# Moving the transposes of q and k behind the output product, with their PSUM banks and waits, in a one-core attention and feed-forward kernel

## What is computed

```python
def _L0_attn_ref(hidden_states, w_qkv, q_ln_w, q_ln_b, k_ln_w, k_ln_b, w_out):   # 128 batches of 32 positions
    qkv = jnp.clip(jnp.einsum('bsd,ed->bse', hidden_states, w_qkv), -8.0, 8.0)
    q, k, v = jnp.split(qkv, 3, axis=-1)
    q, k = _layer_norm(q, q_ln_w, q_ln_b), _layer_norm(k, k_ln_w, k_ln_b)
    ...                                              # 32 heads of 16
    scores = jnp.einsum('bqhd,bkhd->bhqk', q, k) * scale
    probs = jax.nn.softmax(jnp.where(causal, scores + alibi_bias, -inf), axis=-1)
    attn = jnp.einsum('bhqk,bkhd->bqhd', probs, v).reshape(B, S, D)
    return jnp.einsum('bsd,ed->bse', attn, w_out)

x = x + attention(einsum('bct,bcd->bdt', x, style_weights[style_ids]))   # per batch 32x32 mixing first
x = x + ffn(einsum('bsi,boi->bso', x, adapter_weights[adapter_ids]))     # one 512x512 adapter per batch
# ffn: relu(x up)^2 down, plus (sum of the best two gate logits) * x route, then a layer norm
```

## Time and profile before

| | us |
|---|---|
| median of 3 runs | 1124.7 |
| lowest and highest run | 1123.63, 1128.38 |
| the profiled execution, device time | 1129.65 |
| its span (first to last instruction) | 1127.9 |
| TensorE matmuls busy | 1083.4 (96%) |
| weight loads, DVE, ACT, POOL busy | 876.0, 676.3, 600.6, 713.8 |
| mean granted TensorE clock | 0.990 |

### The profile page before, as it was taken

One profiled execution on the slowest core, in us unless ns is written; L12 is line 12 of the kernel. 1 busy time (PEld: TensorE's weight loads), 2 busy tenths in 40 slices (PEclk: granted clock), 3 DMA queues, 4 the chain that ended last, 5 costly groups with the idle time before them and its releaser, 6 DMA issues.

```text
span 1127.9 us, 28302 instructions
## 1 busy us (share of the span) xinstructions
PE 1083.4 (96%) x11396; PEld 876.0 (78%) x11396; DVE 676.3 (60%) x1040; ACT 600.6 (53%) x985; POOL 713.8 (63%) x612
## 2 busy tenths in 40 slices
PE   5999999999999999999989999999999999999994
PEld 3877778788887888788767778787878888787883
DVE  5567667676666667666667245565556565554432
ACT  4466767676766777777767424435261624333220
POOL 4566878788888787878666463556455464433342
PEclk9999999999999999999999999999999999999997
DMA  7125555556554556565567953232414224030101
GB/s 276 41 78 182 183 187 180 169 168 220 173 195 158 198 171 229 170 214 170 175 215 233 350 184 105 84 94 92 126 49 125 67 86 102 28 85 28 47 28 38
DMA packets 95296, 160.84 MB, mean 143 GB/s; under 512 B 46400, under 2 KB 47168, under 8 KB 89792
## 3 DMA queue, kind: packets, MB, share of 16 engines
q1 hardware_dynamic: 79456, 118.16, 32.5%
q0 software_dynamic: 12224, 34.10, 9.5%
q10 hardware_dynamic: 3488, 6.78, 1.7%
HBM read 93.97 MB, written 42.47 MB: 121 GB/s over the span
## 4 chain that ended last, share of the span: by engine, by line
PE 93%; issue 2%; DMA 1%; POOL 1%; DVE 1%; ACT 0%; SPq 0%; POOLq 0%; DVEq 0%; ACTq 0%
PE banks L675 16%; PE banks L860 16%; PE pair L884 15%; PE bank L724 8%; PE bank L675 7%; PE bank L790 7%; PE banks L877 4%; PE bank L877 4%; PE banks L790 3%; PE bank L665 3%; PE pair L692 3%; PE pair L752 2%; PE banks L830 1%; PE banks L735 1%; PE banks L771 1%
## 5 line engine op out<-in xcount | busy, mean ns | idle before, releaser
L1752 POOL TENSOR_TENSOR w_lo<-w2t,w_hi 128x2048 fp32r<-128x2048 f32 x38 | 174.8, 4600 | 39.4 <-ACT w_hi L1053 39.3
L1822 POOL TENSOR_TENSOR u_lo<-act,u_hi 128x512 fp32r<-128x512 f32 x64 | 82.7, 1293 | 102.4 <-ACT u_hi L1253 102.2
L675 PE MATMUL banks<-wqkv_hi,h_hi 128*128 128x512 f32 x256 | 104.7, 409 | 0.2
L860 PE MATMUL banks<-yT_hi,up_hi 128*128 128x512 f32 x256 | 100.8, 394 | 0.0
L675 PE MATMUL banks<-wqkv_hi,h_lo 128*128 128x512 f32 x256 | 100.7, 393 | 0.0
L675 PE MATMUL banks<-wqkv_lo,h_hi 128*128 128x512 f32 x256 | 100.6, 393 | 0.0
L860 PE MATMUL banks<-yT_hi,up_lo 128*128 128x512 f32 x256 | 99.8, 390 | 0.0
L860 PE MATMUL banks<-yT_lo,up_hi 128*128 128x512 f32 x256 | 99.7, 389 | 0.0
L884 PE MATMUL pair<-down_lo,u_hi 128*128 128x512 f32 x256 | 99.6, 389 | 0.0
L884 PE MATMUL pair<-down_hi,u_hi 128*128 128x512 f32 x256 | 99.6, 389 | 0.0
L884 PE MATMUL pair<-down_hi,u_lo 128*128 128x512 f32 x256 | 99.6, 389 | 0.0
(11 more groups left out here) (217 smaller groups left out, 3048.1 us busy)
## 6 DMA issues: line engine op xcount, KB each, us to landing
w2t<-in_w SPq DMA_DIRECT2D x38, 1024.0 KB
vx<-v_hl SPq DMA_DIRECT2D x128, 68.0 KB
x1g<-x_rows SPq DMA_DIRECT2D x32, 256.0 KB, 2.9
kx<-k_hl SPq DMA_DIRECT2D x124, 64.0 KB
x_rows<-x1t SPq DMA_DIRECT2D x31, 256.0 KB, 3.5
ffn_high<-w_high SPq DMA_DIRECT2D x20, 256.0 KB, 3.3
ffn_low<-w_low SPq DMA_DIRECT2D x20, 256.0 KB, 3.4
stage<-in_wqkv SPq DMA_DIRECT2D x3, 1024.0 KB, 8.2
```

The costliest lines, as they stand in the source:

```text
L675: m = e.matmul(into, a[:, c, :], b[:, n, c, :], start=(c == 0 and k == 0), stop=(c == KC - 1 and k == 2))
L860: i = e.matmul((B2, B3)[n % 2], a[:, w, cols], b[m % 2][:, c, :], start=(c == 0 and k == 0), stop=(c == KC - 1 and k == 2))
L1752: e.tensor_tensor(w2_lo[:, :, :], w2t[:, :, :], w2_hi[:, :, :].bitcast(F32), ALU.subtract).then_inc(d_wlo, 1)
L1822: e.tensor_tensor(u_lo[n % FC][:, :], act[n % 2][:, :], u_hi[n % FC][:, :].bitcast(F32), ALU.subtract) \
```

## The change

For the tiles in halves (5 to 29):

- TensorE turns q and k of tile i - 1 behind `out_project(i - 4)` and ahead of `values(i - 3)`.
- The homes in PSUM are exchanged: q and k go to banks47, the slot and the attention's output to banks23. The chunk's detour goes from B4 to B6.
- ACT normalizes q and k later (behind `high_h`), and scales and splits them at the pass's end, k first, with the rounding of the next slot's adapter behind them.
- DVE takes the low parts one pass later, behind the first statistics and ahead of `take_k`; SP spreads k one pass later, behind the spread of v and the store of x1. `low_planes`, `join_planes` and `high_planes` go later in the pass, and SP's stores and loads of planes go behind the load of the adapter.
- `project_q`, `project_k`, `project_v` no longer wait for low parts of q and k in halves; `turn_slot` waits for `ck` (k of tile i is taken out of its bank), `style` waits for the chunk's low part.

TensorE, pass 9, before: steps behind the projections (`xg` is the slot, `on` the attention's output, `w2` the adapter, `wo` the output weights).

```diff
-    turned_values = banks47[:, :, KC * HALF:2 * KC * HALF]
+    turned_slot = half(banks23, 0)
+    turned_values = banks23[:, :, KC * HALF:2 * KC * HALF]
     def q_at(t):
-        return half(banks23, 0) if in_halves(t) else whole(B7 if t == T - 1 else B3)
+        return half(banks47, 0) if in_halves(t) else whole(B7 if t == T - 1 else B3)
...
 SP loop
+                if in_halves(i - 2):
+                    spread_k(i - 2)
                 if 0 <= i - 5 < CHUNKS:
                     keep_chunk(i - 5)
+                if 0 <= i - 4 < CHUNKS:
+                    load_chunk(i - 4)
+                if i >= 5:
+                    load_w2(i - 5)
                 if i >= T - 8:
                     keep_planes(i - T + 8)
...
-                if i >= 1:
+                if i >= 1 and not in_halves(i - 1):
                     spread_k(i - 1)
...
 TensorE
             def project_q(i):
                 upto(e, "cq", i - 1)
-                if in_halves(i - 2):
-                    upto(e, "qlo", i - 2)
-                    upto(e, "klo", i - 2)
+                if i > LAG:
+                    e.wait_ge(d_tl, i - LAG)
+                    upto(e, "olo", i - 5)
...
                 if i >= LAG:
-                    turn_slot(i - LAG, banks47)
+                    turn_slot(i - LAG, banks23)
                 if i >= 4:
                     turn_values(i - 4)
-                if i >= 1:
+                if i >= 1 and not in_halves(i - 1):
                     turn_q(i - 1)
                     turn_k(i - 1)
...
                 if i >= 4:
                     out_project(i - 4)
+                if in_halves(i - 1):
+                    turn_q(i - 1)
+                    turn_k(i - 1)
                 if i >= 3:
                     values(i - 3)
...
 ACT loop
-                if i >= 1:
+                if i >= 1 and not in_halves(i - 1):
                     normalize(i - 1)
...
                 if i >= SHORT:
                     high_h(i + 1)
+                if i >= T - 8:
+                    join_planes(i - T + 8)
+                    high_planes(i - T + 8)
+                if in_halves(i - 1):
+                    normalize(i - 1)
...
                 if i >= 2:
                     soft_exp(i - 2)
+                if in_halves(i - 1):
+                    scale_k(i - 1)
+                    scale_q(i - 1)
+                    high_k(i - 1, k_hl)
+                    high_q(i - 1)
+                    high_w2(i + 1 - LAG)
...
 DVE loop
                 stats_of(i, 0, qn, "cq")
-                if 0 <= i - 5 < CHUNKS:
-                    low_chunk(i - 5)
-                if i >= T - 8:
-                    low_planes(i - T + 8)
+                if in_halves(i - 2):
+                    low_k(i - 2, k_hl)
+                    low_q(i - 2)
                 take_k(i)
                 stats_of(i, 1, kn, "ck")
                 aggregate(i)
+                if 0 <= i - 5 < CHUNKS:
+                    low_chunk(i - 5)
```

More of the change, by code:

```diff
@@ L763, in turn_slot @@
                     e.wait_ge(d_tl, s)
[L764 removed]
+                if slot_halved(s):
+                    upto(e, "ck", s + LAG)
                     upto(e, "olo", s + LAG - 5)
[L766 removed]
+                elif s == LAST:
+                    upto(e, "qlo", T - 3)
+                    upto(e, "klo", T - 3)
                 for c in range(KC):
@@ L770, in turn_slot @@
                             rows = slice(HALF * g, HALF * g + HALF)
-                            m = e.transpose(half(banks47, 0)[:, c, g, :], xg[s % 2][rows, P * c:P * c + P],
+                            m = e.transpose(turned_slot[:, c, g, :], xg[s % 2][rows, P * c:P * c + P],
                                             ident[rows, rows])
@@ L914, in project_k @@
                 upto(e, "ck", i - 1)
-                upto(e, "qhi", i - 2)
-                upto(e, "qlo", i - 2)
+                if not in_halves(i - 2):
+                    upto(e, "qlo", i - 2)
                 project(i, 1, B3, "pk")
@@ L922, in project_v @@
                 upto(e, "cv", i - 1)
-                upto(e, "khi", i - 2)
-                upto(e, "klo", i - 2)
+                if not in_halves(i - 2):
+                    upto(e, "klo", i - 2)
                 if i > LAG:
@@ L929, in turn_q @@
             def turn_q(t):
-                upto(e, "ck", t + 1)
+                if in_halves(t):
+                    upto(e, "qlo", t - 1)
+                    upto(e, "klo", t - 1)
+                    upto(e, "olo", 1)
+                    e.wait_ge(s_routec, KC)
+                else:
+                    upto(e, "ck", t + 1)
                 turn_qk(t, qn[t % 2], "qn", q_at(t), "tq")
@@ L1044, in slot_in @@
                     upto(e, "ot", s + LAG - 4)
-                    e.activation(whole(xgT_hi[:, :]), half(banks47, 0), ACT.Copy).then_inc(d_tc, 1)
+                    e.activation(whole(xgT_hi[:, :]), turned_slot, ACT.Copy).then_inc(d_tc, 1)
                 else:
@@ L1067, in high_chunk @@
                 e.activation(w_high[:, :], w_raw[:, :], ACT.Copy).then_inc(r_high, 1)
-                upto(e, "olo", n)
-                if n + 5 > LAG:
-                    e.wait_ge(d_tl, n + 5 - LAG)
-                e.activation(B4, w_raw[:, :], ACT.Copy).then_inc(r_bank, 1)
+                upto(e, "x1", n)
+                e.activation(B6, w_raw[:, :], ACT.Copy).then_inc(r_bank, 1)
             def fetch(ready, dst, part, first_, count):
@@ L1377, in low_slot @@
                     upto(e, "ohi", s + LAG - 4)
-                    e.tensor_tensor(whole(lo), half(banks47, 0), whole(hi), ALU.subtract).then_inc(d_tl, 1)
+                    e.tensor_tensor(whole(lo), turned_slot, whole(hi), ALU.subtract).then_inc(d_tl, 1)
                 else:
@@ L1588, in _ @@
                     bias_max(i - 2)
-                if i >= 1:
+                if i >= 1 and not in_halves(i - 1):
                     low_q(i - 1)
                     low_k(i - 1, k_hl)
+                if i >= T - 8:
+                    low_planes(i - T + 8)
                 if i >= 4:
```

52 lines of the change are left out of this document (23 added, 29 removed).

## The result

The changed kernel took 1136.9 us (median of five runs, 1133.6 to 1137.9) where the kernel before took 1124.7 (1123.1 to 1128.4): 1.0% slower, ratio 1.0102 with a 95% interval of 1.0077 to 1.0126. The forecast was 1122, with a range of 1111 to 1135, so both the size and the sign were wrong. The profiled execution took 1136.9 us with a span of 1135.1; that is 7.3 us more than the profiled one of before, where the medians are 12.2 us apart: 4.9 us of the difference are in no trace. Two executions further down, one of 1356.6 us (the changed kernel again) and one of 1187.2 us (the adapter's load later), ran at a lower granted clock than their neighbours and are left out of the ratios.

A forecast was written before the change was run, and what follows sets the result against it. The prediction took TensorE's issue, plus stalls from late instruction blocks, as the bound. Terms +3.75 - 9.5 - 1.0 + 2.5 + 0.6 = -3.65 on the profiled 1129.65; for the median it took -2.7: 1122.0 us, range 1111 to 1135.

The forecast's parts named there:

- What bounds the kernel: Attention loop: a pass costs what TensorE issues, 18.30 us; stalls inside steps are late blocks of 256 instructions.
- Late blocks, -9.5: TensorE's stalls: splitting the dense stretch shortens seven stalls, -6.1 us, and ends half-speed windows, -3.4 us.
- Half-speed windows, -3.4: Loop: with stalls below 2 us no half-speed windows follow; two in the loop cost up to 1.7 us each.
- The switch, +3.75: From k's transposes to the values: a new change of tile shape, 0.15 us in each of 25 passes.
- The adapter's low part, -1.0: Passes 24 to 30: the adapter is rounded at the end of the pass before, taking away waits, -1.0 us.
- k late, +2.5: Scores: the spread of k in time to 1.2 us late; 0.1 us a pass taken for single late ones.
- The first rival: Scores wait for kx in every pass: at 0.7 us a pass, 17.5 in place of 2.5, 1137 us; chance 0.17.
- The stalls only move: Blocks cut elsewhere but as many come late: the -9.5 falls away, the switch stays, about 1130 us; chance 0.16.
- The queues, cost 0: SP's, DVE's and ACT's work delayed by the change in their queues: costs 0 while the named margins stand.
- The tail, +0.6: Pass 31: DVE comes free about as far from the pass's start, so 0, up to +1.7 for a half-speed window.
- Profiled against median: A median run, 4.95 us under the profiled one, probably has fewer stalls to shorten: a third of the 9.5 goes.

The follow-up runs named there:

- the changed kernel again: The changed kernel, unaltered, run a second time: 1137.4 us, ratio 1.0086 to the kernel before.
- the adapter's load later: The changed kernel with the adapter's load issued only when the transposes of q are done: 1176.5 us, ratio 1.0465.
- the second traces: Traces of both kernels run again without edit: the kernel before 1129.7 us profiled, the changed kernel 1137.4 us measured.
- the run with an eighth of the adapter: The changed kernel loading 128 KB in place of 1 MB of the adapter for slots 1 to 25: 1133.2 us, ratio 1.0046.
- the three alignments: The changed kernel unshifted, and with 64 or 168 instructions of one-column products ahead of the loop: 1136.9, 1151.9 and 1151.1 us.
- the shift of 64: The changed kernel with 16 products of one column, 64 instructions, ahead of the loop: 1151.9 us, ratio 1.0213.
- the shifted kernel before: The kernel before with 16 products of one column, 64 instructions, ahead of the loop: 1123.0 us, ratio 0.9964.
- shift 168: The changed kernel with 42 products of one column, 168 instructions, ahead of the loop: 1151.1 us, ratio 1.0205.
- The last run: The kernel before with 16 one-column products ahead of the loop and, in passes 24 to 30, the adapter rounded ahead of the planes: 1120.8 us, ratio 0.9949.
- the kernel before shifted by waits: The kernel before with 128 satisfied waits, 64 instructions, ahead of TensorE's first product: 1125.1 us, ratio 0.9983.

## Why the prediction was wrong, point by point

**What bounds the kernel: right.** A clean pass is TensorE's issue, 18.32 us, and stalls inside steps are late blocks of 256 instructions. That was the ground of the argument, and the borders come out in every trace.

**Late blocks, -9.5: the step that failed.** The term was 6.1 us less for shorter stalls and 3.4 less for the stretches of half the clock. By the two windows TensorE was idle for 12.2 us of the loop before and 10.3 after, and in the second traces for 11.4 and 12.9: no less in sum. And the same 7310 matmuls kept it busy for 4.7 us more (4.2 in the second traces). Of this the stretches of half the clock, 6.8 us longer in sum (3.4 in the second traces), can make up to half their length, 3.4 and 1.7 us, and the switch 0.5; the rest I can't place. So the 6.1 came out near 0, and the 3.4 turned into up to 3.4 us more. The prediction said: "with the values they make 112 pairs, but 12 wide ones stand ahead of them", and so looked for density in the scores alone; and from 4.5 us against some 5.1 it concluded that a stall would shrink to 0.6 to 0.8. It counted the time of a block from its first instruction, so that wide products at its head counted as time in which the next one could come. In pass 11 the block starts at 209.10 us with 36 instructions of wide products, and its successor's packet starts only at 214.06, 4.96 us later; in the run with an eighth of the adapter it is 5.1 us, though no data had been in flight for 2 us. What is left behind the wide products is 33 instructions of q's and k's turns and 187 of the values, and these run from 212.86 to 214.27: 1.4 us, where 3.5 pass until TensorE can go on. Before, the values (192 instructions, 1.07 us in the earlier trace rows) stood between wide products and could never use up 220 alone. So the change made a second dense stretch. That it thinned the first is not shown: the scores' stalls were 7.4 and 5.9 us in the two traces of before and 4.9 and 7.1 in the two of the changed kernel.

The experiments with the shifts bear this out. At each of the three alignments of the changed kernel the values of two passes stall (216 and 422; 314 and 533; 249 and 457 us), and at the shift of 64 also the first projection behind them (256 and 470); in the kernel before the first stall of over 0.5 us in the values comes at the end of pass 30 or later. But only at the first alignment is density shown to be enough. For the stalls at 314 and 533 the count of theory F gives nothing: the packets start 6.6 and 8.3 us into their blocks, at 312.0 and 531.0 us, where the adapter's load and, at 531, the planes' transfers had filled the DMA engines. For those at 249 and 457 it gives 1.2 us each, where 2.5 and more were measured.

**Half-speed windows, -3.4 in that term: they went the other way.** The forecast had them end with stalls under 2 us. The loop has three such stretches, one of them twice as long, in place of two. Nor does the length of the idle time alone decide. The clock fell to 0.50 behind 1.82 us without a matmul at 323.1 us and behind 2.17 us at 216.8 (the changed kernel again), and did not behind 1.99 us at 393.1 (the shifted kernel before), 2.47 us at 249.4 (the changed one, shift 168), 2.66 us at 255.9 (shift 64) and 2.88 us at 479.4 (the changed kernel again). Two windows of that last trace, behind 479.4 and behind 323.1 us (length, PE busy, ..., granted clock):

```profile
479.50:482.50 3.00, 2.99 (x15) 2.40 (x15) 2.78 (x4) 0.00 (x0) 1.34 (x2) 1.00 0.07 16
324.10:327.51 3.41, 3.41 (x9) 2.67 (x8) 1.85 (x3) 0.00 (x0) 2.61 (x3) 0.50 0.43 118
```

**The switch, +3.75: too high.** k's turns to the values took the 0.40 us that was forecast:

```profile
290.09 0.33 PEld L742 LDWEIGHTS banks<-cst,kn 64*128 64x128 f32 x8
290.49 0.10 PEld L698 LDWEIGHTS pair<-vx,p_hi 128*32 128x32 bf16 x4
...
291.42 0.19 PEld L681 LDWEIGHTS banks<-wqkv_hi,h_hi 128*128 128x128 f32 x1
```

The values themselves took 0.93 in place of 1.07 (327.94 to 329.01 in the earlier trace rows), so that a pass is 0.02 us longer and all 25 are 0.5. Why the step is shorter behind small matmuls is open.

**The adapter's low part, -1.0: right.** No product in passes 25 to 30 waits for it. The last run took this wait away without the rest of the change.

**k late, +2.5: too high in the loop.** kx is issued at +5.1 us as forecast, and in passes 6 to 30 costs 0.8 us in sum. (The spread of v takes 3.1 us there and not under 3; the margin covered it.) The first rival, k late in every pass, gave nearly the right time (1137) for a reason that didn't occur.

**"The stalls only move", chance 0.16:** nearest to what happened, but it had no cost of its own beyond the switch; here the stalls moved and grew.

**The queues, cost 0: wrong in one point.** Each margin that was named held. Not named was that kx's spread now flies at +5 to +9 us of a pass, beside gathers, store and planes, while blocks are asked for. The load of the adapter did not move (+13.0 us of a pass), but under it now lies a dense stretch. In the run with an eighth of the adapter 4 us went, but not at the stalls in the values; what the spread costs was not tried.

**The tail, +0.6: too low by some 3.5 us.** "DVE comes free at about the same distance from the pass's start" failed. ACT now scales and splits q and k and rounds adapter and probabilities ahead of the last planes, whose high part starts 7.9 us into pass 31 (586.64) where it was 2.3 (578.73). Where no late block hides it, this is seen plainly, as in the changed kernel shifted by 64:

```profile
600.42 2.51 DVE L1453 TENSOR_TENSOR y_low<-y_word,y_high 128x512 fp32r<-128x512 f32 x1 [2.71 <-ACT y_high L1114]
...
605.17 0.66 PE L744 MATMUL bank<-cst,kn 128*128 128x128 f32 x4 [3.78 <-DVE vf L1388]
```

In the kernel before the same wait, by its waits of TensorE between 470 and 605 us, was shorter:

```profile
PE bank L737 <- DVE vf L1364: 1.2, 1, 1.2
```

In the unshifted kernel a late block (2.5 us) and kx (1.9 us) stand in its place, and taking kx's share away gave 0.9 us back. The Trainium skill ("SBUF — State Buffer", Who interferes with whom) has a DVE instruction of two SBUF inputs contend with a GpSimd instruction that reads SBUF. The row agrees: it takes 2.51 us, from 600.42 us, beside the adapter's low part on POOL (597.80 to 602.38), where the median of this line is 0.68.

**Profiled against median.** The forecast took an execution of before at the median to have fewer stalls. Both profiled ones took 1129.7, in comparisons whose medians are 1124.7 and 1128.2, 1.5 to 5 us above. But the profiled executions of the shifted kernel before (1121.2 and 1120.1) lie 3 to 4 us under their medians, and that of the changed kernel on its median, so this is spread between executions and no cost of profiling that could be taken off. Of the 12.2 us between the medians the traces explain 7.3.

**What stays open:** which share of the changed kernel's loss in passes 24 to 30 is transfers and which is density (the count of theory F gives 0.7 us for the stall of 2.7 in pass 24), what sets the start of a block's packet, and why about half of the places that the count names do not stall in the kernel before.

The Trainium skill ("Runtime: NRT & Kernel Launch", Instruction fetch mechanics) says that the sequencer fetches the next 16 KB while it runs the current block, and that this is mostly hidden. The first half agrees with the packets and with the borders of 256. The second doesn't hold here: up to 6.0 us at one border. By the page, a shift of the instructions would move neither kernel; it moved them by -0.4% and by over +1%.

## What to carry to other kernels

Where TensorE runs small matmuls, count instructions as well as time: where most of a block of 256 ran in less than about 3.6 us, as 220 did in 1.4 us here, TensorE could stall at the block's border (about half of such places did in the kernel before). Moving small steps next to other small ones makes such a stretch, even if the busy time stays the same. Compare two orders at more than one alignment of the blocks (some idle instructions ahead of the loop): a single one showed 12 us here where the others showed 13 and 29. And where a kernel has few such stretches, the alignment itself is worth a run: 64 instructions ahead of the loop gave 0.4% here.

## What the runs showed of the hardware

- TensorE's instructions come in blocks of 256, a packet of 16 KB each. At a late block TensorE goes on 2.2 to 2.5 us after the packet's start in most stalls, even with no other transfer in flight (214.38 to 216.72 us with an eighth of the adapter). The packet's start is at no fixed place of the block before: it was 4.96 us and 210 instructions in at pass 11, 11 instructions in behind the stall at 583.4 us. Beside busy DMA engines the idle time reached 6.0 us (470.2 us, shift 64).
- Stalls repeat at the same instructions from run to run (216 and 422 us twice in the changed kernel, 210 and 361 us twice before), but not all of them do (323 us, once in two traces).
- A wait whose semaphore is set already is not free: 64 instructions of such waits, from 5.78 to 12.60 us in the kernel before shifted by waits, started 0.11 us apart and held TensorE's first product back by 5 us.
- The granted clock was 0.50 behind an idle time of 1.82 us (323.1 us, the changed kernel again) and not behind one of 2.88 us (479.4 us, the same trace).
- 42 products of one column ahead of the loop, with the granted clock at 0.50 for 14 to 17 us, delayed it by 14 us; 16 of them by 1 to 1.5.
